# Recurrent block with a Strassen feed-forward on eight cores: one quadrant of four leaves the chip at a stage change, sums are spread, the first layer follows the norm, residual inputs are fetched ahead

## The reference, cut to what matters

```python
xn = layernorm(x)                       # over 1024 features, eps 1e-5
# random features: weights and feats share proj_matrix (1024 x 1024)
rfs(v) = exp(xi) / 32 * exp(xi * (v @ proj.T) - 0.5 * |v|^2 * xi^2)
s = rfs(xn) @ rfs(input_weights).T      # 1024 outputs
h = silu((xn @ w1.T) * w1_s) * ((xn @ w2.T) * w2_s)       # 1024 -> 4096
h = gelu((h @ h1.T) * h1_s)             # 4096 -> 4096
h = gelu((h @ h2.T) * h2_s)             # 4096 -> 4096
g = silu((h @ w3.T) * w3_s)             # 4096 -> 1024
y = x + s * g
```

## Time and profile before

| what | us |
|---|---|
| three timed runs | 2542.61, 2714.05, 2872.23 |
| their median | 2714.05 |
| profiled execution, its own time | 2538.48 |
| its span on the slowest core (core 1) | 2537.4 |
| spans of the eight cores | 2517.9 to 2537.4 |
| TensorE busy on core 1 | 2386.9 (94%) |
| VectorE, ScalarE, GpSimd busy | 1136.2, 397.1, 225.4 |

### The profile page before, as it was taken

One profiled execution on the slowest core, in us unless ns is written; L12 is line 12 of the kernel. 1 busy time (PEld: TensorE's weight loads), 2 busy tenths in 40 slices (PEclk: granted clock), 3 DMA queues, 4 the chain that ended last, 5 costly groups with the idle time before them and its releaser, 6 DMA issues.

```text
span 2537.4 us, 29788 instructions; the slowest of 8 cores (2517.9 to 2537.4 us)
## 1 busy us (share of the span) xinstructions
PE 2386.9 (94%) x10832; PEld 1067.0 (42%) x10832; DVE 1136.2 (45%) x1309; ACT 397.1 (16%) x568; POOL 225.4 (9%) x406
## 2 busy tenths in 40 slices
PE   3999999999899999999857999999999999999988
PEld 1444444444344444444312444444444444444433
DVE  5333443444643443564622233443443554344476
ACT  1112111111111111112302221111111111111111
POOL 2000000001000100002011000000000000000000
PEclk8999999999999999999968999999999999999989
DMA  6444356556645556768032444345546654554694
GB/s 102 79 79 75 58 92 110 91 97 105 138 87 102 102 90 107 148 107 131 20 75 87 90 77 75 59 88 101 103 88 109 151 90 89 103 101 89 132 225 112
DMA packets 87902, 251.56 MB, mean 99 GB/s; under 512 B 9552, under 2 KB 29136, under 8 KB 86480
## 3 DMA queue, kind: packets, MB, share of 16 engines
q0 software_dynamic: 57376, 192.96, 46.0%
q1 hardware_dynamic: 30384, 56.71, 7.1%
HBM read 414.26 MB, written 28.31 MB: 174 GB/s over the span
## 4 chain that ended last, share of the span: by engine, by line
PE 83%; DVE 8%; DMA 6%; issue 1%; POOL 1%; ACT 1%; DVEq 0%; SPq 0%; ACTq 0%; POOLq 0%
PE pb L156 83%; DMA blk<-xT 3%; DMA wring<-w3p 1%; DMA wring<-h2p 1%; POOL blk L627 1%; DVE blk L257 1%; DVE blk L254 1%; DVE tmp L547 1%; DVE blk L460 1%; DVE wring L318 1%; DVE blk L457 1%; DVE blk L448 1%; ACT blk L551 0%; POOL blk L212 0%; ACT stg L690 0%
## 5 line engine op out<-in xcount | busy, mean ns | idle before, releaser
L156 PE MATMUL pb<-blk,wring 128*128 128x512 bf16 x10112 | 2206.0, 381 | 72.0 <-ACT blk L411 36.8
L156 PEld LDWEIGHTS pb<-blk,wring 128*128 128x128 bf16 x10112 | 993.3, 98 | 1284.6 <-issue 107.1
L318 DVE TENSOR_TENSOR wring<-wring 128x2048 bf16<-128x2048 bf16 x216 | 264.7, 1226 | 54.8 <-DVE tmp L372 16.0
L295 DVE SCALAR_TENSOR_TENSOR blk<-pb,cols,stg 128x512 bf16<-128x512 f32 x128 | 96.1, 751 | 290.1 <-PE pb L156 250.2
L420 ACT ACTIVATE stg<-pb,cols 128x512 bf16<-128x512 f32 x120 | 82.5, 687 | 794.7 <-DVE tmp L365 629.6
L156 PE MATMUL pb<-blk 128*128 128x512 bf16 x640 | 159.3, 412 | 50.4 <-DVE tmp L624 36.1
L325 DVE TENSOR_TENSOR wring<-wring 128x2048 bf16<-128x2048 bf16 x144 | 176.4, 1225 | 15.3 <-DVE wring L318 0.5
L411 ACT ACTIVATE blk<-tmp,cols 128x512 bf16<-128x512 f32 x128 | 92.4, 722 | 367.4 <-DVE tmp L391 194.3
L290 ACT ACTIVATE stg<-pb,cols 128x512 bf16<-128x512 f32 x128 | 87.9, 687 | 357.8 <-PE pb L156 355.0
L182 POOL DMA_DIRECT2D wring<-h1p x128 | 67.7, 529 | 753.6 <-PE pb L156 753.6
L365 DVE TENSOR_TENSOR tmp<-pb,tmp 128x512 f32<-128x512 f32 x72 | 49.8, 692 | 189.2 <-PE pb L156 188.1
(11 more groups left out here) (72 smaller groups left out, 434.8 us busy)
## 6 DMA issues: line engine op xcount, KB each, us to landing
wring<-h1p POOLq DMA_DIRECT2D x128, 512.0 KB, 6.0
wring<-h2p POOLq DMA_DIRECT2D x128, 512.0 KB, 5.9
wring<-w12p POOLq DMA_DIRECT2D x64, 512.0 KB, 5.3
wring<-w3p POOLq DMA_DIRECT2D x32, 512.0 KB, 7.9
blk<-xT SPq DMA_DIRECT2D x32, 256.0 KB, 5.2
y<-blk SPq DMA_DIRECT2D x32, 256.0 KB, 2.5
spill0h<-stg SPq DMA_DIRECT2D x60, 128.0 KB, 2.0
blk<-spill0h SPq DMA_DIRECT2D x4, 1920.0 KB, 15.4
```

Source lines behind the costliest of these rows:

```text
L156: ii = t.matmul(p[bk], lhs, rhs, start=(not onto and i == 0), stop=(i == n - 1), skip_group_check=onto)
L295: a = V(lambda: v.scalar_tensor_tensor(kt(h[q], row), p[b2], w2s_c[:, oc:oc + 1], stg[:, ts_, :], op0=ALU.mult, op1=ALU.mult), m2, a)
L318: tok = V(lambda: v.tensor_add(wring[:, so, :], wring[:, slots[ka][0], :], wring[:, slots[kb][0], :]), *toks, slots[ka][1], slots[kb][1])
```

## The change

At a stage change only quadrant 12 goes through HBM; 21 gets a block of its own (`out21`), which was the block that kept the normalised x. The normalised x of sweep 0 is written to HBM after the norm (`xn_hbm`) and read back after u4 of the last row group of h2. The sums are placed otherwise: M1 after u2, M4 after u3, M7 after u6, M3 after u0 and M6 after u1 of the next stage's first row group (`late`). In `w12_stage` each operand has its own token, the sums are in the order of use, and the first four chunks run feature pair by feature pair behind the norm, in all eight banks at once. The norm's squares move to ScalarE, two chunks each; its loads are 4 DMAs a half; center and divide are separate and, in the middle part, placed between the exponentials. The residual loads of the y part are issued ahead into 16 places, and the last layer finishes each output one emit later.

```diff
 def ln_squares(th, b, bq, *toks):
-    for j in range(8):
-        ln[th, "sq"] = V(lambda j=j: v.tensor_mul(xq[:, j, cs], xb[:, j, cs], xb[:, j, cs]), ...)
+    for jj in range(4):
+        js = slice(2 * jj, 2 * jj + 2)
+        ln[th, "sq", jj] = S(lambda: sc.activation(xq[:, js, cs], xb[:, js, cs], AF.Square),
+                             ln[th, "x", jj], *toks)
 def ln_scale(th, f0, f1, f2):
-    a = V(lambda: v.tensor_copy(f0, p[bm]), ln[th, "m"])
-    a = V(lambda: v.tensor_mul(f1, p[bm], f0), a)
-    a = V(lambda: v.tensor_sub(f1, p[bv], f1), a, ln[th, "q"])
+    a = S(lambda: sc.activation(f1, p[bm], AF.Square), ln[th, "q"])
+    c = V(lambda: v.tensor_sub(f1, p[bv], f1), a)
+    a = V(lambda: v.tensor_copy(f0, p[bm]), a)
...
 def w12_stage(s_, xnb, bl, after_chunk, *toks):
     def sums(i):
+        ops_ready["M2"] = hv["11", i]
+        ops_ready["M5"] = hv["22", i]
+        ops_ready["M1"] = V(...)      # then M4, M7, M3, M6, each with its own token
+    for th in range(2):
+        bk = [take_bank() for _ in range(8)]
+        for jj in range(4):
+            need(t, ln[th, "xn", jj])
+            for i in range(4):
+                need(t, slots[key(i)][1])
+                for w in range(2):
+                    for k in (2 * jj, 2 * jj + 1):
+                        ii = t.matmul(p[bk[2 * i + w]], wtile(key(i), 8 * w + k), xn[:, k, cs],
+                                      start=(k == 0), stop=(k == 7))
+        for i in range(4):
+            gate(i, th, bk[2 * i], toks_[2 * i], bk[2 * i + 1], toks_[2 * i + 1])
+    for i in range(4, 32): ...        # as before
...
 row_group:
+    def edge_(u, m):
+        edge(u, m)
+        for fn in late.pop(u, ()):
+            fn()
 hidden_stage:
-    nb = {"M2": o11, "M5": o22, ..., "M7": bl["M2"], "M3": bl["M7"], "M6": bl["M5"], ...}
+    nb = {"M2": o11, "M5": o22, ..., "M7": o21, "M3": bl["M5"], "M6": bl["M2"],
+          "out21": bl["M7"], "out11": bl["M3"], "out22": bl["M6"]}
     edge_last:
+    u == 0: end["r12"] = d_rel.inc(sy.dma_start(most(nb["M6"]), spill[s_, nm][:, 0:15, :]), 16)
+    u == 2: V(M1 = o11 + o22, rows 0-14)
+    u == 3: V(M4 = o21 - o11, rows 0-14)
+    u == 6: V(M1 row 15); V(M4 row 15); ops_ready["M7"] = V(o21 += o22, whole)
+            late[0] = [sum_m3]        # M3 = M6 - o22, rows 0-14, then row 15
+            late[1] = [sum_m6]        # M6 += o11, whole
...
 first norm:
+S(lambda: sc.activation(tmp[:, 0, 0:1], c_eps, AF.Ln), ones_tok)
+ln_scale(0); ln_center(0, .., 0); then ln_center(jj), ln_divide(jj - 1) for jj = 1..3
+ln_squares(1); ln_stats(1); ln_divide(0, 3); ln_scale(1); centers and divides of half 1
+ln_extra(0); ln_extra(1)
+xn_out = d_xn.inc(sy.dma_start(xn_hbm, blk[:, b_xn, :]), 16)
...
 middle part:
+need(sy, end["u4"], xn_out)           # in the last row group of h2
+xn_tok = d_xn.inc(sy.dma_start(blk[:, fr3, :], xn_hbm), 16)
+feats(0, fr3, xn_tok)
+iw squares (V); ln_squares(0) (S); f_last = feats(1, fr3); ln_squares(1) (S)
+for n_ in range(8): x_load(n_, s_, f_last)
+ln_stats(0); ln_stats(1); column sums of iw
+need(sc, qt[1]); need(v, qt[1]); ln_scale(0); ln_scale(1); copies of the column sums
     for rc in range(8):
         for oh in range(2): ... expo(...)
+        ln_center(rc // 4, b_x, ftl, rc % 4)
+        ln_divide(rc // 4, b_xn1, ftl, rc % 4)
+ln_extra(0); ln_extra(1)
+for n_ in range(8, 16): x_load(n_, s_, m)
     for n_, (oc, th) in enumerate(y_at):   # y part, no load in it, 16 places xf[n_]
...
 last layer of sweep 1:
+for n_ in range(8): x_load(n_, end["u4"])
+need(sy, end["u5"], end["u6"], now(d_s))
+sr = two loads of s_hbm (2048 KB each)  # before: these two first, then the x loads
     emit: silu, then finish() of the emit before (mul, add, store of y)
```

More of the change, by code:

```diff
@@ L224, in ln_stats @@
             cs = slice(th * N, (th + 1) * N)
[L225 to L229, removed]
+            need(t, ones_tok)
+            bm, bv = take_bank(), take_bank()
+            for j in range(8):
+                need(t, ln[th, "sq", j // 2])
+                t.matmul(p[bm], ones_d, xb[:, j, cs], start=(j == 0), stop=(j == 7))
+                ii = t.matmul(p[bv], ones_d, xq[:, j, cs], start=(j == 0), stop=(j == 7))
+            ln[th, "q"] = cT.inc(ii)
             ln[th, "banks"] = (bm, bv)
@@ L240, in ln_scale @@
[L240 to L250 removed]
+            ln[th, "mean"] = a
+            a = S(lambda: sc.activation(f2, f1, AF.Ln, bias=c_eps[:, 0:1]), c, ones_tok)
@@ L287, in w12_stage @@
                     b2 = take_bank()
-                    m2 = mm_group(b2, [(wtile(key, 8 + k), xn[:, k, cs]) for k in range(8)])
-                    ts_ = (2 * i + th) % 4
-                    a = S(lambda: sc.activation(stg[:, ts_, :], p[b1], AF.Silu,
-                                                scale=w1s_c[:, oc:oc + 1]),
-                          m1, gate_free.get(ts_), now(d_stg[ts_]), col_tok)
-                    free_bank(b1, a)
-                    q = str(half + 1) + str(th + 1)
@@ L295, in w12_stage @@
[L295 to L303 removed]
+                    m2 = mm_group(b2, [(wtile(key(i), 8 + k), xn[:, k, cs]) for k in range(8)])
@@ L304, in w12_stage @@
+                    gate(i, th, b1, m1, b2, m2)
+                give_slot(key(i), m2)
+                if i % 2 == 1:
+                    sums(i // 2)
                 after_chunk(i)
-            for q in ("M2", "M5", "M1", "M4", "M7", "M3", "M6"):
-                ops_ready[q] = ops_ready["all"]
         gate_free = {}
@@ L671, in where, with x_load, finish @@
                             slice(s_ * TS + th * N, s_ * TS + (th + 1) * N), oc, th)
-                def x_load(n_):
+                def x_load(n_, *toks):
+                    q, r = order[n_]
+                    rows, cs, oc, th = where(q, r)
+                    need(sy, *toks)
+                    x_tok[n_] = d_xf[n_ % 8].inc(sy.dma_start(xf[:, n_ % 8, :], xT[rows, cs]), 16)
+                for n_ in range(8):
+                    x_load(n_, end["u4"])
+                need(sy, end["u5"], end["u6"], now(d_s))
+                sr = [d_sr[i].inc(sy.dma_start(f32b(b), s_hbm[:, 8 * i:8 * i + 8, :]), 16)
+                      for i, b in enumerate((fr1, fr2))]
+                done = [0]
+                owed = []
+                def finish():
+                    if not owed:
+                        return
+                    n_, gi, a = owed.pop(0)
                     q, r = order[n_]
```

341 lines of the change are left out of this document (182 added, 159 removed).

## The result

| what | us |
|---|---|
| changed kernel, four timed runs | 2439.11, 2442.96, 2501.59, 2852.86 |
| their median | 2472.28 |
| kernel before, four runs, median | 2628.33 (2541.98 to 2872.23) |
| changed kernel, profiled execution | 2439.11 |
| ratio to before, 95% interval | 0.9602 (0.956 to 0.9643) |

A second comparison on another occasion, in five rounds, gave medians of 2438.07 and 2535.15 over all executions and 2436.10 in the profiled one, a ratio of 0.9614 (0.9601 to 0.9627).

What follows compares the result with a forecast made beforehand. TensorE was taken as the bound: 10832 matmuls, 2335 us at dense pace, 202 idle or at the lower clock. Savings of 16 + 13 + 41.5 + 56 - 2 = 124.5 from 2538.5 gave 2414 us, range 2390 to 2455.

Steps and rivals of the forecast that it cites:

- the last layer of sweep 1: Last layer: short waits of 2.2 us go, tail grows 0.9, s_hbm comes later; 2 us lost (15 lost to 4 won).
- xn in sweep 0: Change h2 to w3: 2 MB of xn share the engines with the last tile, delaying s5; 1 us.
- executions longer than the profiled one: Whole kernel: 175 us in the earlier median of 2714 that no trace row shows; neither they nor their absence forecast.
- the s_hbm term: Last layer: s_hbm, issued behind 2 MB of x, costs some 5 us idle and 2 cold instead of 2.0 and 1.8.
- The start: First norm and first w12 matmuls: weights end last, 31 us lost instead of 47; 16 saved (12 to 20).
- w12 to h1: Stage change in both sweeps: the 3.7 us wait and its cold stretch go; 13 us saved.
- h1 to h2: Stage change: 1.4 us lost per change, 1.1 idle and 0.3 for s2 of row group 1, no cold stretch.
- The middle: From w3's end through the y part and sweep 1's w12: 60 us minus 4, 56 saved (45 to 62).
- The wait at the stage changes only shrinks: Rival 1: 7 us kept at each of four changes, 10 more at the s_hbm reads; 2452 us, chance 0.15.
- loads still pace the y part: Rival 2, y part: SP's queue or DMA engines hold the loads, so its 62 us gain goes; 2476, chance 0.06.
- The third: Rival: VectorE's rounds cheaper or TensorE stays warm, short new waits absent; 2400 or below, to 2392 us, chance 0.12.
- The fourth: Rival, dense stretches: fewer pauses lower the granted clock; over 2% slower from 0.93 (2590), 2732 at 0.88; chance 0.03.

Runs made afterwards that it cites:

- e1: Changed kernel with the two s_hbm loads issued ahead of the eight x loads at the last stage change; 2424.07 us.
- e3: Changed kernel with sweep 0's normalised x read back later, from u3 of w3's second row group; 2434.71 us.
- e5: Changed kernel with one more 1920 KB transfer, HBM to HBM and read by nobody, after u1 at each of four stage changes; 2478.32 us.
- e6: Changed kernel, one quadrant through HBM, with M1 after u3, M4 after u4, and M7, M3 and M6 all after u6; 2459.39 us.
- e4: Changed kernel with the y part's residual x loads back inside its loop, one ahead of each chunk, still 16 places; 2481.04 us.
- e7: Changed kernel with w12_stage's first four chunks taken one by one as before, one bank at a time; 2435.59 us.

## Why the prediction was wrong, and where it was right

**The step that failed in the kernel: the last layer of sweep 1.** "It took 22.6 and arrives about 26.5 after u6's end; ... some 5 idle and 2 cold." It took 32.6 and 38.0 and cost 17.9 idle and 1.7 cold. I had seen the mechanism, s behind 2 MB of x on one queue, and the sum s2 behind its product, but took the 22.6 of a load that left at once and added 4 us for the x before it. For 2 MB of x, with the weight tiles beside them, that was too little: in e1, where s goes first, the second of the two loads took 20.7 instead of 38.0, and the wait is 3.4. This one term is half of the 25 us: 19.6 where 7 stood.

**The second, smaller one: xn in sweep 0, "s5 then waits until 14 to 17 where 14.3 is free; 1 us".** The row is 4.9 idle and 2.7 cold, 5.2 above the forecast's part, and e3 removes it. It is the same error: a transfer of 2 MB was priced by the slack of the one behind it and not by its share of the engines. The change at 2316 has its like in the x loads (1.65, and 1.6 in two short waits); in e1, where they are issued later, the 1.65 is gone.

**The step that put the median outside the range: executions longer than the profiled one, put at nothing.** The range was built around the profiled execution, and the sentence "I forecast neither them nor their absence" left out of it whatever lifts a median above that. The median of four lies between 2442.96 and 2501.59, and the range ended at 2455; a range that leaves such a part out of its sum has to reach over it. The three runs before had already been 4, 176 and 334 us above the profiled one. The profiled execution, 2439, lies in the range; with the s_hbm term right the median would still be some 2460. Why some executions are longer stays open.

**Right, by the rows.** The start: 32.2 lost, forecast 31; but for another reason than mine, so the number is luck. No weight tile ends a wait there. The tiles are issued from 7.39, not from 10.02 as I had kept from before, since there are only four x loads a half ahead of them on POOL. The first pass starts when the eighth bank is free, behind the second half's copy (L243), and ended at 46.9 where I had 48.5 by the tiles. The pass of the second half waits 3.1, forecast 2.3, and is 3 us cold. w12 to h1: no wait, twice. h1 to h2: 1.7 and 2.0, forecast 1.4: 0.8 ahead of u6 where I had 1.1, 0.45 for s2 of row group 1 where I had 0.3, and 0.4 and 0.8 ahead of u5, where I had nothing; e5 shows the tile behind the transfer and e6 the queue of sums, so the two things that the prediction's layout of VectorE sets against each other are both real. The middle: the y part starts behind 14.97 idle, forecast 14.5, 2.4 cold against 2.3, the last exponential 2.08 against 2.1, the two waits of sweep 1's first layer 0.93 and 3.07 against 0.7 and 2.3. A Square of 1024 columns took 1.06, taken as 1.1.

**The rivals.** The first ("The wait at the stage changes only shrinks") held at one of the four changes, h2 to w3 in sweep 0 with 7.6 where it had 7, and its second half did, "10 more at the s_hbm reads": the two were one case in my text and need not be. The second (loads still pace the y part) is ruled out: no wait on L692 is left, and e4 shows what it looks like. The third's spared waits did not come. The fourth, a granted clock below 1.00 in the dense stretches, is ruled out for this execution. The limit of 13/16 that the prediction names there stands in the Trainium skill, TensorE: Matmul & The Clock Gate, in the section Seeing it yourself, and the next window, at 1.00, does not show it either. The window over a long stretch (columns: TensorE, weight loads, VectorE, ScalarE, GpSimd, then clock, DMA share and GB/s) shows 1577 matmuls in 340 us at 1.00, as in the earlier trace rows:

```profile
690.00:1030.00 340.00, 340.00 (x1577) 154.16 (x1576) 149.87 (x156) 47.67 (x70) 29.71 (x56) 1.00 0.55 96
```

## What to carry to other kernels

A load put ahead of another on one queue must be charged with its whole size against what stands behind it, and that with what stands behind its reader on the engine: here 2 MB of x cost 15 us, and swapping the two groups of loads gave them back. When a tile and a queue of sums stand one behind the other, list what is late next before pricing either: moving the sums beside a second transfer left 52.1 us of waits at the stage changes, taking the transfer away alone 32.5, both together 11.9. Fitting the matmuls to the norm gained 1 us of the start's 15, and issuing loads ahead of their loop gained 46.5 of the 64.7 of the y part and `feats`. And a small effect is read from its rows: waits elsewhere and the clock moved the time of one execution by as much as e3's and e7's edits were worth.

## What the hardware showed that I had not expected

SP issued two loads of 2048 KB in 0.80 us with an idle queue (e1) and in 3.48 behind eight others; eight loads of 256 KB took 9.23 and 10.22. The DMA engines were about equally busy on all cores between 2310 and 2330 (a share of 0.94 to 1.04), but moved different amounts, 185 to 296 GB/s. In the windows below (stretch, us, matmuls where shown, granted clock, DMA share, GB/s) the last two are of cores 4 and 1:

```profile
1044.00:1048.00 4.00, 3.73 (x9) 0.50 1.06 160
...
1327.00:1331.00 4.00, 3.33 (x16) 1.00 0.00 0
...
2320.00:2330.00 10.00, 1.00 0.96 192
...
2320.00:2330.00 10.00, 1.00 0.99 288
```

TensorE's wait for s was 14.7 to 18.9 us on five cores and 5.4 to 11.1 on three; in the repeat (3.6 to 16.4) the cores that waited long were in part others. With s first it was 3.4 on all eight, and their spans lay within 9 us of one another instead of 20. Why the rate differs stays open.

And the clock: behind 4.88 us without work the granted clock is 0.50 (1.2 GHz) in the row at 1044, behind 3.07 it is 1.00 in the row at 1327. But the same wait at the same place of the same execution went the other way on core 1, the first row below (as on cores 2, 3, 5 and 7): 64 matmuls took 15.66 where core 4 had 13.97. Even behind 2.08, which cost nothing in the changed kernel, e1 has a granted clock of 0.50 on core 4 after more than 50 us of matmuls at 1.00, the second row:

```profile
1321.59 15.66 PE L316 MATMUL pb<-blk,wring 128*128 128x512 bf16 x64 [3.07 <-DVE blk L297]
...
1278.79 29.46 PE L157 MATMUL pb<-blk 128*128 128x512 bf16 x128 [2.08 <-ACT blk L609]
```

At the start, behind 3.10, the granted clock is 0.51 and 64 matmuls took 16.86 on core 4; 13.8 is the dense time. A wait of two or three microseconds costs 0 to 3 us of clock, and the rows do not say when. Such stretches are one part of what makes two executions of one kernel differ by some microseconds.
